# Graph attention over 8192 nodes: one in four casts of the adjacency matrix moves from ScalarE to GpSimd

## The reference

```python
h = jnp.maximum(_layernorm(x, axis=-1), 0.0)
Wh = h @ W_w + W_b
e = jax.nn.leaky_relu((Wh @ a1)[:, None] + (Wh @ a2)[None, :], negative_slope=0.2)
attention = jnp.where(adj > 0, e, NEG)
attention = jax.nn.softmax(attention, axis=1)
x = x + attention @ Wh
```

## Time and profile before

| | |
|---|---|
| device time, median of 3 runs | 1673.91 us (1673.81 to 1674.71) |
| the profiled execution, its own time | 1675.64 us |
| its span in the trace | 1673.8 us |
| TensorE busy | 1523.4 us (91%) |
| VectorE busy | 1504.4 us (90%) |
| ScalarE busy | 1512.5 us (90%) |
| GpSimd busy | 44.0 us (3%) |
| mean granted TensorE clock | 0.965 of full speed |
| DMA | 300.75 MB, mean 180 GB/s |

### The profile page before, as it was taken

How to read it: one execution, slowest core, us unless ns; L and a number is a source line. 1 busy time by engine, 2 the same in 40 slices (tenths; PEclk the granted TensorE clock), 3 DMA queues, 4 the chain that set the end, 5 groups by cost and what they waited for, 6 DMA issues and landing times.

```text
span 1673.8 us, 32554 instructions
## 1 busy us (share of the span) xinstructions
PE 1523.4 (91%) x12228; PEld 1304.5 (78%) x12228; DVE 1504.4 (90%) x1157; ACT 1512.5 (90%) x1223; POOL 44.0 (3%) x72
## 2 busy tenths in 40 slices
PE   3865898979998999979998999979998999979998
PEld 2754787768886888868886888868887788868887
DVE  4647999998999899998999899998999899998996
ACT  3668999979999799979999799988999799988993
POOL 0540000000000000000000000000000000000000
PEclk9987999989999999989999999989999999989999
DMA  9509999898999899998999899998999899998980
GB/s 202 115 10 199 199 172 172 162 208 160 212 192 196 176 207 197 190 200 164 211 193 194 178 205 199 190 197 167 213 191 199 174 206 198 189 193 167 213 153 26
DMA packets 301952, 300.75 MB, mean 180 GB/s; under 512 B 17504, under 2 KB 296672, under 8 KB 301792
## 3 DMA queue, kind: packets, MB, share of 16 engines
q1 hardware_dynamic: 301792, 298.55, 94.0%
HBM read 290.06 MB, written 8.42 MB: 178 GB/s over the span
## 4 chain that ended last, share of the span: by engine, by line
PE 58%; ACT 27%; issue 8%; DVE 5%; DMA 1%; POOLq 0%; SPq 0%; ACTq 0%; DVEq 0%; POOL 0%
PE acc L671 45%; ACT work L349 10%; ACT adj_rows L337 9%; PE acc L675 9%; ACT work L362 6%; PE acc L647 3%; DVE work L557 1%; ACT X L369 1%; DVE adj_cols L500 1%; DMA work<-in_x 1%; PE acc L639 1%; DVE xr L586 1%; DVE work L565 1%; DVE xr L452 1%; POOLq L64 0%
## 5 line engine op out<-in xcount | busy, mean ns | idle before, releaser
L671 PE MATMUL acc<-X,work 128*128 128x257 f16 x10752 | 1240.7, 275 | 15.5 <-DVE work L565 15.5
L671 PEld LDWEIGHTS acc<-X,work 128*128 128x128 f16 x10752 | 1049.5, 98 | 191.6 <-DVE work L565 19.0
L557 DVE SCALAR_TENSOR_TENSOR work<-work,adj_cols 128x2048 f32<-128x2048 f32 x256 | 579.4, 2284 | 53.8 <-ACT work L349 44.2
L349 ACT ACTIVATE work<-q_bc,r_j 128x1024 f32<-128x1024 f32 x512 | 550.8, 1135 | 51.1 <-PE acc L675 51.1
L565 DVE SCALAR_TENSOR_TENSOR work<-work,sigma 128x2048 f16<-128x2048 f32 (+1 forms) x256 | 530.8, 2074 | 24.7 <-ACT work L362 24.7
L337 ACT ACTIVATE adj_rows<-adj_rows 128x2048 bf16<-128x2048 int32 x256 | 479.1, 1896 | 8.2 <-DMA adj_rows<-in_adj 8.2
L362 ACT ACTIVATE work<-work,sigma 128x2048 f16<-128x2048 f32 (+1 forms) x256 | 454.6, 1776 | 25.9 <-DVE work L557 25.7
L500 DVE STREAM_TRANSPOSE adj_cols<-adj_rows 128x1024 int32<-128x1024 int32 x256 | 311.1, 1233 | 15.0 <-ACT adj_rows L337 3.1
L675 PE MATMUL acc<-X,work 128*128 128x257 f32 x1024 | 241.5, 380 | 0.0
L675 PEld LDWEIGHTS acc<-X,work 128*128 128x128 f32 x1024 | 184.9, 190 | 22.7
L686 PE MATMUL acc<-mean_wh,tiny 128*128 128x257 f16 x64 | 21.7, 339 | 93.5 <-DVE xr L586 62.6
(11 more groups left out here) (64 smaller groups left out, 83.3 us busy)
## 6 DMA issues: line engine op xcount, KB each, us to landing
adj_rows<-in_adj SPq DMA_DIRECT2D x1024, 256.0 KB, 8.1
work<-in_x SPq DMA_DIRECT2D x16, 512.0 KB, 19.7
xr<-in_x SPq DMA_DIRECT2D x16, 512.0 KB, 12.8
out<-xr SPq DMA_DIRECT2D x16, 512.0 KB, 11.6
q_bc<-q_rows SPq DMA_DIRECT2D x8, 512.0 KB, 12.2
q_bc<-in_L_gnn_W_w SPq DMA_DIRECT2D x2, 128.0 KB, 2.1
xr<-in_L_gnn_a SPq DMA_DIRECT2D x2, 128.0 KB, 5.9
q_bc<-in_L_gnn_W_b SPq DMA_DIRECT2D x1, 128.0 KB, 4.2
```

Source lines behind the costliest of these rows:

```text
L349: ins = nc.scalar.mul(Wt[:, i, e, :], q_bc[:, odd, :], r_j[:, 2 * k + e:2 * k + e + 1])
L557: nc.vector.scalar_tensor_tensor(out=Wt[:, i], in0=Wt[:, i], scalar=1.0, in1=edges, op0=ALU.max, op1=ALU.min).then_inc(s_M, 1)
L671: return nc.tensor.matmul(acc[:, m, 0:F1], Et[:, i, 1 if k == 2 else 0, e, m * P:(m + 1) * P], X16[:, 2 * (CW * c + i) + e, 1 if k == 1 el ...
```

## The change

The cast of set 3 of each chunk is taken off ScalarE's order and put on GpSimd as a `tensor_scalar` (greater than zero, times the same huge number). It has a semaphore of its own, `s_castp`; ScalarE's `s_cast` now counts three casts a chunk. The transpose of set 3 and the reload of the buffer of set 3 wait for `s_castp`. GpSimd's cast waits for the load of set 3 and for the transpose of set 1, which frees the buffer that it writes.

```diff
+            def slot_read(s, n):
+
+                c = n // SETS - 1
+                if n % SETS == SETS - 1:
+                    sp.wait_ge(s_castp, NC * s + (c + 1))
+                else:
+                    sp.wait_ge(s_cast, (SETS - 1) * NC * s + ((SETS - 1) * c + n % SETS + 1))
+
             for n in range(NAT, NSET):
-                sp.wait_ge(s_cast, n - NAT + 1)
+                slot_read(0, n)
                 load_adj(0, n)
...
             nc.gpsimd.partition_all_reduce(top[:, :], ext[:, :], P, RMAX).then_inc(s_top, 1)
 
+            for s in range(NS):
+                for c in range(NC):
+                    m = SETS - 1
+                    pool.wait_ge(s_nat[m], 16 * NQ * NC * s + 16 * NQ * (c + 1))
+                    pool.wait_ge(s_T, NSET * s + (SETS * c + m - 1))
+                    nc.gpsimd.tensor_scalar(rows16[:, m % 2], nat[:, m], 0.0, BIG, ALU.is_gt, ALU.mult).then_inc(s_castp, 1)
...
                 if not end:
                     cast(nx[0], nx[2], 2)
-                    cast(nx[0], nx[2], 3)
...
-            for m in range(2, SETS):
-                cast(0, 0, m)
+            cast(0, 0, 2)
             cast(0, 1, 0)
...
             def transpose(s, c, m, first=False):
 
-                dve.wait_ge(s_cast, NSET * s + (SETS * c + m + 1))
+                if m == SETS - 1:
+                    dve.wait_ge(s_castp, NC * s + (c + 1))
+                else:
+                    dve.wait_ge(s_cast, (SETS - 1) * NC * s + ((SETS - 1) * c + m + 1))
```

More of the change, by code:

```diff
@@ L162, in gat_layer @@
         s_cast = sem("adj_cast")
+        s_castp = sem("adj_cast_by_pool")
         s_T = sem("adj_transposed")
@@ L230, in super_row @@
                 for n in range(NSET):
-                    sp.wait_ge(s_cast, NSET * s + (n - NAT + 1))
+                    slot_read(s, n)
                     load_adj(s, n)
```

## The result

The changed kernel takes **1916.33 us** (median of 4 runs, 1914.81 to 1919.59) against 1674.31 us for the kernel before in the same runs: ratio 1.1446, 95% interval 1.1426 to 1.1466. It is 242 us slower. The forecast was 1839 us with a range of 1727 to 1915; the direction and the mechanism came as forecast, the size didn't, and the time lies 1.3 us outside the range.

The account below looks back on a forecast made before the run. Three engines within one per cent bound the kernel, none with slack. Terms 136.8 + 10.5 + 20 - 3.5 = 163.8 us on 1675.64 gave 1839 us, range 1727 to 1915.

Parts of the forecast that it names:

- What bounds the kernel: Per chunk VectorE needs 21.9 us, TensorE 22.05, ScalarE 22.24; no engine has slack worth naming.
- The contention: VectorE instructions with two SBUF operands, such as low 2, cannot run beside GpSimd's cast; whichever issues first holds the port.
- The order: GpSimd's cast starts some 0.15 us ahead of low 2, which is held until the cast ends; chance 0.52.
- the rival without contention: Cast beside low 2 hides whole up to 3.5 us: 1675 us, chance 0.10; a long cast 1726 us, chance 0.05.
- D: Length of GpSimd's cast of 2048 elements per partition: 3.0 us, between 2.0 and 4.3.
- 48 chunks within super rows: Super rows 2 to 8: low 2 begins later by D - 0.15 = 2.85 us each, 136.8 us.
- 7 first chunks: First chunk of super rows 2 to 8: finish 0 runs beside the cast, leaving 1.5 us each, 10.5 us.
- first super row: Eight casts: two short two-operand instructions follow transpose 1; between 2.0 and 3.0 us each, taken as 2.5, 20 us.
- change of super row: Half of ScalarE's wait at a super row's end is given back, 7 x 0.5 = 3.5 us; TensorE's second half moves along unchanged.
- ScalarE's relief: ScalarE loses one cast a chunk, some 1.8 us, booked at nothing because TensorE and VectorE cover it.
- an unchanged clock inside the chunks: With TensorE idle 3 us in 25, its granted clock was expected to stay the same as the first super row's 0.97.
- The rival with VectorE first: Low 2 gets the port first, transpose 3 then waits about D - 1.0 = 2.0 us: 1795 us, chance 0.30.

Follow-up runs that it names:

- the run beside: Kernel before, all casts on ScalarE, with GpSimd making two unused 1024-element tensor_scalar per chunk in super rows 2 to 8: 1687.64 us, ratio 1.0071.
- its own run: Changed kernel with GpSimd's cast waiting also for low 2, so that VectorE comes first in every chunk: 2061.53 us, one run.
- The fastest version: Kernel before with both read-out halves moved ahead of weights 3 of the next super row's first chunk, TensorE's super rows written out: 1626.57 us, ratio 0.9714.

## Why the prediction was right and wrong

**Right.** What bounds the kernel: three engines within a per cent, so that relief buys little. The contention, read from two collisions of a fraction of a microsecond in the preparation, holds for low 2. The rule of the Trainium skill (SBUF — State Buffer, Who interferes with whom) agrees as to who is hit: two SBUF inputs are held, a transpose and a reading from PSUM are not, and writing alone holds nobody. Where it lets the first to issue keep the port to its end, the trace agrees for VectorE, which frees it 0.13 or 0.14 us before its end in the two collisions shown, and differs for GpSimd: the cast frees it 2.80 us before its end. The order came as forecast, GpSimd in the gap of 0.33 us ahead of low 2. And the rival without contention, 1675 us, is refuted by the run beside.

**The step that failed: D.** The prediction took one number for the cast's length and the hold, 3.0 us between 2.0 and 4.3. The length is 7.08 us and the hold 4.28, so the upper bound didn't hold. It was drawn from an addition with two inputs as the dearest thing in the trace, 2.0 ns per element; a tensor_scalar with two operations takes 3.37, the slope from 1024 to 2048 elements. The number of inputs was the wrong measure. The comparison accounts for 0.84 ns of the 3.37, and whether the input is int32 or f32 changes nothing (3.63 us for 1024 elements of either); what makes up the other 2.5 ns no run shows. The second fault in the same step is that the hold isn't the length at all. The two nearly cancel: the hold happens to equal the upper bound of 4.3, so the sum there, 1921 us, lies near the truth by chance.

The terms, against the profiled executions (1917.41 - 1675.64 = 241.8 us):

| term | forecast | measured |
|---|---|---|
| 48 chunks within super rows | 48 x 2.85 = 136.8 | 48 x (26.09 - 22.24) = 184.8 |
| 7 first chunks | 7 x 1.5 = 10.5 | 7 x 2.77 = 19.4 |
| first super row | 8 x 2.5 = 20 | 8 x (28.77 - 25.04) = 29.8 |
| change of super row | -3.5 | the rest, +7.8 |

In the first row a hold of 4.28 us would by the forecast's formula cost 4.13, and 3.85 came: the difference, 0.28, is ScalarE's relief as VectorE feels it. 0.22 of it can be seen: transposes 2 and 3 take 2.36 us, where with a short wait for ScalarE's cast between them they took 2.58. That relief is the second thing I undersized, at nothing. The run without any cast of set 3 put it at 6 us in all, because TensorE's pace caps it there; in the changed kernel VectorE is far behind TensorE and gets it in full, some 13 us over 48 chunks. In the third row the two short instructions behind transpose 1 take 5.08 us together, where they took 0.84. One by one, and the cast beside them:

```profile
183.67 0.45 DVE L592 SCALAR_TENSOR_TENSOR X<-X,c_j 128x257 f16<-128x257 f32 x1
...
184.03 4.72 DVE L592 SCALAR_TENSOR_TENSOR X<-X,c_j 128x257 f16<-128x257 f32 x1
```

```profile
183.90 7.15 POOL L293 TENSOR_SCALAR adj_rows<-adj_rows 128x2048 bf16<-128x2048 int32 x1 [21.61 <-DVE adj_cols L517]
```

The first runs in its usual time; the cast gets in between the two, and the second is held. It costs 4.24 us, less 0.20 of idle time that goes and the relief; the forecast had 2.5.

The last row has the wrong sign. I let TensorE's second half "move along, unchanged", but behind the second stop the clock is down again, and VectorE's waits after it are 0.77 and 6.61 us instead of 6.14, which over seven super rows makes 8.7 us. No run isolates this. The forecast of an unchanged clock inside the chunks was wrong too: TensorE stops for 3.86 us ahead of 892.83, and from 892.40 to 895.70 the granted clock is 0.50. That cost nothing there, since TensorE had room.

**The rival with VectorE first** had the same fault: at D - 1.0 it would have paid 6.1 us, not 2.0, and been the slower of the two, as its own run shows. The price of waiting is the length, and 7.08 us can't hide behind low 2 and one transpose.

**The range** ended at 1915, 6 us short even of the sum at its own upper bound, and that bound took the dearest row of the trace for a limit on an operation that no row shows. A bound beyond the rows needs more room than one between them.

**Open.** Why the hold of 2048 elements ends 2.80 us before the cast's end (1.93 us with one operation), while 512 and 1024 elements hold for 0.40 and 0.83 us, 0.8 ns per element. At 3.37 and 2.53 ns per element these ends are 830 and 760 elements. GpSimd reading some 800 elements ahead of its arithmetic would give all four holds within about 0.1 us; it is argued, not shown, and no size between 1024 and 2048 was tried. The fastest version, with the moved read-out and the written-out loop, was not tried with less work on ScalarE. Starting the cast where VectorE idles for another reason, as in the 6.6 us of a super row's second chunk, was not tried.

## What to carry to other kernels

Before moving work to an idle GpSimd, look for which VectorE instructions will stand beside it and how many of their operands lie in SBUF, and in the profile of the changed kernel look at the lengths of VectorE's instructions, not at its idle time. Price such work from a row of the same operation at two sizes, not from another operation, and keep apart how long it shuts VectorE out from how long its result takes. When three engines stand within a per cent of each other, taking work off one of them buys little; look for the places where all of them stop. Here the change of super row was worth 48 us, and the cast, taken away altogether, 6.

## What the hardware showed that I had not expected

- A GpSimd tensor_scalar takes 1.92, 3.63 and 7.08 us for 512, 1024 and 2048 elements per partition with two operations, and 5.36 us for 2048 with one; int32 and f32 input are alike.
- It lets VectorE's instruction with two SBUF operands in before it ends: after 0.40, 0.83, 4.28 and, with one operation, 3.43 us. The other way round, a cast that comes second is let in only 0.13 or 0.14 us before VectorE's instruction ends. Cutting the cast into pieces lets VectorE in between and lengthens the whole, from 7.08 to 8.31 us.
- The instruction that is shut out is recorded as busy from its start: 6.46 us for low 2 instead of 2.35, 3.86 for a cast instead of 1.92.
- TensorE stood 6.8 us at the jump back of a loop of some 1500 matmuls, with no wait to show for it but two packets of instructions arriving; behind the stop the granted clock was 0.50, behind the written-out loop's stop of 2.44 us it was 1.00.
